# Layer 3 taken ahead of layer 2 as six 512-column products, a copy to rows and eight fp32 transposes, with the tile conversions in two pieces

## The chip, the cores and the metric

The kernel runs on one core of one Trainium2 chip. The metric is the device time of one execution in microseconds (us), and lower is better.

## The reference, cut to what is computed

32 batches of 64 rows and 1024 features go through four residual layers. Two of them are linear layers with a low-rank (LoRA) term, the third multiplies by one of eight 1024x1024 matrices, the fourth mixes the 64 rows of a batch by one of sixteen 64x64 matrices:

```
x = x + (x @ W0.T + b0 + scale[id] * (x @ A0[id].T) @ B0[id])     # ids 1 to 7
x = x + (x @ W1.T + b1 + (x @ A1[id].T) @ B1[id])                 # ids 6 to 15
x = x + x @ W2[id].T                                              # 1024x1024, ids 3 to 7
x = x + einsum('bct,bcd->bdt', x, W3[id])                         # 64x64 on the rows, ids 0 to 15
```

The third layer ("layer 2" in the kernel, counted from 0) acts on features and the fourth ("layer 3") on rows, so the two can be done in either order.

## The kernel before, in words

**Prologue (0 to about 165 us).** Layers 0 and 1 are fused: the product M of their weights, the coupled LoRA tables and the bias are computed once. The batches are sorted by their layer 2 matrix, and tables in SBUF say which batch, LoRA and matrix comes when.

**Pairs.** 16 pairs of batches (128 rows each) follow. Every fp32 operand of a large product is split in a high and a low fp32r part, and a product is three matmuls (hi*hi, hi*lo, lo*hi; `SPLIT`). A 1024-wide result needs two banks of 512 columns, so a product over 8 feature tiles is 8*3*2 = 48 matmuls of 512 columns. For pair j TensorE (PE) does:

- `low_products(j)` (L1056, 8 matmuls of 256 columns): both LoRA A products;
- `main_part(0)` (L1064, 24 matmuls);
- `between_loras(j)` (L1071, one matmul): the first LoRA's contribution to the second's low-rank input. It waits for `low_ready` (the split sums of the first LoRA, DVE L819 to L839) and `g_ready` (`couple`, DVE L807);
- `main_part(1)` (24 more) and `lora_b(j)` (L1079 and L1080, 4 matmuls). `lora_b` waits for the second LoRA's sums (DVE L852 to L839, the second chain). Then `y_done(j)`;
- `layer2(j-1)`: first half (L1101, 24 matmuls with tiles 0 to 3 of the matrix in `ring`), then `transposes(j)`, then the second half (24, tiles 4 to 7).

`transposes(j)` (L1092) does layer 3 and the transpose in one: the stationary operand is a 128x128 block of the split x2, the moving one the 128x128 W3, so 8 blocks * 3 parts = 24 matmuls of 128 columns write `t_ps`, which is already transposed as layer 2 wants it. `x2` is layer 1's output: DVE adds the bias (`take_x2`, L864, after `y_done`), ACT casts the high part (`x2_hi`, L565), DVE the low part (`x2_lo`, L872). The result is split again, half by half: `xs2_hi` (ACT L559), `xs2_lo` (DVE L868).

**The ring.** `ring` holds the current matrix, split, 8 tiles. When the next pair takes the next matrix (`following`), ACT and DVE convert its tiles (`convert`, ACT L547, DVE L859) from a stage of four slots, tiles 0 to 3 in `step(j)` (after layer 2's first half is used) and tiles 4 to 7 in `step(j+1)`. SyncE (SP) loads tile k of 4 to 7 (L277) when the low part of tile k-4 is converted, and in its queue the next pair's loads stand behind them: x (L246), LoRA A (L255), LoRA B (L264 to L267), W3 (L272). The matrix changes four times: three times between pairs (`following`) and once inside a pair (`mixed`).

**Order.** Each engine has its program written by hand, in order; waits are on semaphores. ACT in `step(j)`: `take_out(j-2)`, `xs2_hi(j-1, 1)`, tiles 4 to 7 if due, `a_hi(j+1)` (L527, needs the LoRA A load), `split_w3(j)` (L571), `x_hi(j+1)` (L520, two), `x2_hi(j)`, `b_hi_parts(j+1)` (L534, L535, and the copies L538 and L541, which raise `b_again`), mixed tiles, `xs2_hi(j, 0)`, tiles 0 to 3 if due. DVE follows the same order with its low parts, and the LoRA sums of pair j stand at the start of its step.

## Time and profile before

| | us |
|---|---|
| median of 3 runs | 619.14 (618.62 to 619.67) |
| the profiled execution | 617.97 |
| its span, first to last instruction | 616.2 |
| PE, matmuls busy | 598.6 (97%) |
| PE, weight loads busy | 496.5 (81%) |
| DVE busy | 304.2 (49%) |
| ACT busy | 263.9 (43%) |

"Busy" of PE is the time with a matmul in flight. Matmuls overlap: one of 512 columns is shown with about 390 ns, but the next starts about 230 ns after it. A late matmul is therefore read from the distance of two starts, and the idle time in brackets behind a row is shorter than the delay.

### The profile page before, as it was taken

Reading aid. Unit: us, or ns where it says so; the run is one execution under the profiler, and the core shown is the slowest. Engines: PE = TensorE matmul, PEld = TensorE weight load, DVE = VectorE, ACT = ScalarE, POOL = GpSimd, SP = SyncE. Lnnn points to the kernel's source line nnn. Section 1 sums busy time; section 2 is a strip of 40 time slices with the busy share of each in tenths; the row PEclk is TensorE's granted clock in tenths of the full one; section 3 lists DMA queues with packets and bytes.
Section 4 is the critical chain, followed back from the end, with each engine's and each line's share of the span. In section 5 each row is a group of like instructions: output and inputs, shape, how many; then the busy total and the mean of one; then the engine's idle time right before and its main releaser. Section 6 shows DMA issues by size and latency. Waiting matters only on the chain.

```text
span 616.2 us, 10822 instructions
## 1 busy us (share of the span) xinstructions
PE 598.6 (97%) x2870; PEld 496.5 (81%) x2871; DVE 304.2 (49%) x547; ACT 263.9 (43%) x337; POOL 56.6 (9%) x87
## 2 busy tenths in 40 slices
PE   8999999999989999999999899999999998999997
PEld 7888878888878887888888788888878874888885
DVE  6993220031686368453545845454584563535320
ACT  5632211033485184544527553552755372345111
POOL 3240001000012002000200200020021001000000
PEclk9999999999989999999999999999999997999999
DMA  8646723010054125423121642312164242021102
GB/s 312 236 170 68 86 87 139 18 52 17 2 207 158 53 48 194 172 70 98 41 68 36 204 172 70 98 41 68 36 204 172 70 155 84 17 87 36 36 1 69
DMA packets 66012, 60.92 MB, mean 99 GB/s; under 512 B 42050, under 2 KB 50242, under 8 KB 65988
## 3 DMA queue, kind: packets, MB, share of 16 engines
q1 hardware_dynamic: 65988, 60.63, 33.1%
q8 instruction: 11, 0.18, 0.1%
q14 instruction: 13, 0.11, 0.1%
HBM read 49.33 MB, written 11.27 MB: 98 GB/s over the span
## 4 chain that ended last, share of the span: by engine, by line
PE 79%; issue 6%; DVE 5%; ACT 4%; DMA 2%; ACTq 1%; DVEq 1%; POOL 1%; SPq 0%; POOLq 0%
PE y_ps L1064 22%; PE y_ps L1101 22%; PE y_ps L1018 11%; PE t_ps L1018 5%; PE t_ps L1092 5%; DVE ring L859 2%; PE y_ps L999 2%; PE low_ps L1056 2%; DMA arena<-wt 2%; ACTq L224 1%; PE y_ps L995 1%; PE t_ps L999 1%; PE low_ps L999 1%; ACT ring L547 1%; DVE arena L864 1%
## 5 line engine op out<-in xcount | busy, mean ns | idle before, releaser
L1101 PE MATMUL y_ps<-ring,ops 128*128 128x512 f32 (+1 forms) x792 | 190.3, 396 | 7.1 <-DVE ring L859 4.2
L1101 PEld LDWEIGHTS y_ps<-ring,ops 128*128 128x128 f32 (+1 forms) x792 | 145.8, 186 | 44.4 <-issue 7.9
L1064 PE MATMUL y_ps<-wm,ops 128*128 128x512 f32 x768 | 180.5, 393 | 0.0
L1064 PEld LDWEIGHTS y_ps<-wm,ops 128*128 128x128 f32 x768 | 142.7, 189 | 29.3 <-DVE arena L864 0.2
L1018 PE MATMUL y_ps<-ring,wm 128*128 128x512 f32 x240 | 55.3, 390 | 0.0
L859 DVE TENSOR_TENSOR ring<-arena,ring 128x1024 fp32r<-128x1024 f32 x40 | 48.9, 1271 | 12.2 <-ACT ring L547 12.0
L1018 PEld LDWEIGHTS y_ps<-ring,wm 128*128 128x128 f32 x240 | 44.9, 188 | 9.3
L520 ACT CAST ops<-arena 128x512 fp32r<-128x512 f32 x32 | 19.4, 620 | 70.3 <-PE y_ps L1064 70.3
L547 ACT CAST ring<-arena 128x1024 fp32r<-128x1024 f32 x40 | 40.4, 1049 | 15.9 <-POOL arena L431 15.8
L1092 PEld LDWEIGHTS t_ps<-w_split,ops 128*128 128x128 f32 x384 | 45.9, 194 | 1.2
L431 POOL TENSOR_TENSOR arena<-arena,ident 128x128 f32<-128x128 f32 x40 | 24.5, 622 | 236.6 <-DMA arena<-wt 233.3
L1092 PE MATMUL t_ps<-w_split,ops 128*128 128x128 f32 x384 | 45.4, 275 | 0.0
L577 ACT COPY arena<-y_ps 128x1024 f32<-128x1024 f32 (+1 forms) x17 | 16.4, 964 | 67.4 <-PE y_ps L1101 40.8
L868 DVE TENSOR_TENSOR ops<-t_ps,ops 128x512 fp32r<-128x512 f32 x32 | 22.0, 691 | 45.6 <-ACT ops L559 45.1
L783 DVE TENSOR_TENSOR ops<-arena,ops 128x512 fp32r<-128x512 f32 x32 | 21.7, 687 | 31.9 <-ACT ops L520 31.9
L435 POOL TENSOR_TENSOR w_stage<-w_stage,ident 128x128 f32<-128x128 f32 x16 | 14.2, 886 | 241.1 <-DMA w_stage<-w 241.1
L565 ACT CAST ops<-arena 128x1024 fp32r<-128x1024 f32 x16 | 16.8, 1050 | 45.0 <-DVE arena L864 45.0
L819 DVE TENSOR_TENSOR low_a<-low_ps,low_mask 64x128 f32<-64x128 f32 x32 | 9.2, 288 | 51.7 <-PE low_ps L1056 51.2
L538 ACT CAST ops<-arena 32x1040 fp32r<-32x1040 f32 x32 | 33.9, 1059 | 0.6
L541 ACT CAST b_split<-arena 32x1024 fp32r<-32x1024 f32 x32 | 33.4, 1044 | 0.6
L1018 PE MATMUL t_ps<-ring,wm 128*128 128x512 f32 x144 | 33.3, 390 | 0.0
L1018 PEld LDWEIGHTS t_ps<-ring,wm 128*128 128x128 f32 x144 | 27.0, 188 | 5.6
(142 smaller groups left out, 565.6 us busy)
## 6 DMA issues: line engine op xcount, KB each, us to landing
arena<-wt SPq DMA_DIRECT2D x48, 512.0 KB, 4.6
arena<-xt SPq DMA_DIRECT2D x32, 256.0 KB, 2.8
out<-arena SPq DMA_DIRECT2D x30, 256.0 KB, 3.1
arena<-w SPq DMA_DIRECT2D x8, 576.0 KB, 5.3
a_stage<-a_tab SPq DMA_DIRECT2D x64, 64.0 KB, 1.9
arena<-b_tab SPq DMA_DIRECT2D x64, 64.0 KB, 2.0
arena<-a_cols SPq DMA_DIRECT2D x8, 256.0 KB, 4.1
a_tab<-bias SPq DMA_DIRECT2D x4, 256.0 KB, 8.5
```

The lines of the kernel that those rows point to most:

```text
L431: nc.gpsimd.tensor_tensor(diag, diag, ident[:, :], ALU.add).then_inc(w_folded, 1)
L538: op = nc.scalar.copy(b0_split[group(0, g), :], b0_stage[group(0, HI), :])
L541: op = nc.scalar.copy(b1_split[group(1, g), :], b1_stage[group(1, HI), 0:FEATS])
L547: nc.scalar.copy(ring[:, k, 0, :], w_stage[:, k % STAGES, :]).then_inc(w_hi, 1)
L783: nc.vector.tensor_tensor(xs_of(h, 1), x_of(h), xs_of(h, 0), ALU.subtract).then_inc(x_lo_ready, 1)
L859: nc.vector.tensor_tensor(ring[:, k, 1, :], w_stage[:, k % STAGES, :], ring[:, k, 0, :], ALU.subtract).then_inc(w_lo, 1)
L868: nc.vector.tensor_tensor(xs2_of(h, 1), t_of(h), xs2_of(h, 0), ALU.subtract).then_inc(xs2_lo_ready, 1)
L999: op = nc.tensor.matmul(PASS1[i], wm[:, i, part_w, k * P:(k + 1) * P], a1[:, k, part_a, :], start=False, stop=k == KT - 1 and part_w == 1)
L1018: op = nc.tensor.matmul(to[:, cols], left(part_w, k), ring[:, k, part_r, cols], start=k == 0 and part_w == part_r, stop=k == KT - 1 and pa ...
L1064: op = nc.tensor.matmul(y_ps[:, cols], xs[:, k, part_x, :], wm[:, k, part_w, cols], start=k == 0 and part_x == part_w, stop=False)
L1092: op = nc.tensor.matmul(t_ps[:, cols], x2_split[:, part_x, cols], w3_split[:, part_w, :], start=part_x == part_w, stop=part_x == 1)
L1101: op = nc.tensor.matmul(y[0:m, cols], xs2[:, k, part_x, 0:m], ring[:, k, part_w, cols], start=k == 0 and part_x == part_w, stop=k == KT - ...
```

## The change

PE takes layer 3 as a product of its own ahead of the second half of layer 2: W3 is the stationary operand and x2 the moving one, 2 banks * 3 parts = 6 matmuls of 512 columns (`layer3`). Its result stands in rows; ACT copies it to SBUF as fp32 (`take_x4`, into the place of x2), and eight fp32 transposes of PE bring it into `t_ps`. These stand ahead of the last tile's matmuls of layer 2. The copies that raise `b_again` are a function of their own and move behind `xs2_hi(j, 0)` on ACT; `couple` moves into the next step on DVE. Of tiles 4 to 7, tile 4 is converted ahead of the second LoRA chain's end and tiles 5 to 7 behind it. The first two pairs have an order of their own. SP and GpSimd are as before.

```diff
@@ scalar
-                for g in (A_LO, LOW_LO):
-                    op = nc.scalar.copy(b0_split[group(0, g), :], b0_stage[group(0, HI), :])
-                op.then_inc(b_again, 1)
...
+            def b_again_parts(layer):
+
+                split, stage = ((b0_split, b0_stage), (b1_split, b1_stage[:, 0:FEATS]))[layer]
                 for g in (A_LO, LOW_LO):
...
+                    op = nc.scalar.copy(split[group(layer, g), :], stage[group(layer, HI), :])
                 op.then_inc(b_again, 1)
...
+            def take_x4(j):
+                act.wait_ge(l3_done, j + 1)
+                nc.scalar.copy(x4, t_ps[:, :]).then_inc(x4_ready, 1)
...
+            def first_half_of_next(j):
+                rank, mixed, following = first_rank(act, j), mixed_of(act, j), following_of(act, j)
+                with act.If(following != 0):
+                    act.wait_ge(half_used, j + 1)
+                    convert(rank + mixed + 1, FIRST_HALF)
...
+            def second_step():
+                a_hi(2)
+                convert(0, (6, 7))
+                x_hi(2, 0)
+                take_x4(0)
+                x_hi(2, 1)
+                for h in range(2):
+                    xs2_hi(0, h)
...
+            def step(j, last=False):
+                take_out(j - 2)
+                xs2_hi(j - 1, 1)
+                second_half_of_next(j - 2, SECOND_HALF[:1])
                 if not last:
                     a_hi(j + 1)
...
                 split_w3(j)
+                second_half_of_next(j - 2, SECOND_HALF[1:])
...
                 x2_hi(j)
                 if not last:
                     b_hi_parts(j + 1)
...
+                take_x4(j)
+                behind_layer2(j - 1)
                 xs2_hi(j, 0)
...
+                if not last:
+                    for layer in range(2):
+                        b_again_parts(layer)
+                first_half_of_next(j - 1)
@@ vector
             def take_x2(j):
                 dve.wait_ge(y_done, j + 1)
+                if not (isinstance(j, int) and j == 0):
+                    dve.wait_ge(t_done, j)
...
+            def step(j, last=False):
+                sum_low(j, 0)
+                split_low(j, 0)
+                couple(j)
+                sum_low(j, 1)
+                xs2_lo(j - 1, 1)
+                second_half_of_next(j - 2, SECOND_HALF[:1])
+                finish_low(j)
                 if not last:
                     a_lo(j + 1)
...
                 split_w3(j)
+                second_half_of_next(j - 2, SECOND_HALF[1:])
...
                 take_x2(j)
                 x2_lo(j)
                 if not last:
                     b_lo_parts(j + 1)
...
+                behind_layer2(j - 1)
                 xs2_lo(j, 0)
...
+                first_half_of_next(j - 1)
@@ tensor
+            def layer3(j):
...
+                for cols in BANKS:
+                    for part_x, part_w in SPLIT:
+                        op = nc.tensor.matmul(t_ps[:, cols], w3_split[:, part_w, :], x2_split[:, part_x, cols],
+                                              start=part_x == part_w, stop=part_x == 1)
+                op.then_inc(l3_done, 1)
+
+            def transposes(j):
+                pe.wait_ge(x4_ready, j + 1)
                 for k in range(KT):
                     cols = slice(k * P, (k + 1) * P)
...
+                    op = nc.tensor.transpose(t_ps[:, cols], x4[:, cols], ident[:, :])
                 op.then_inc(t_done, 1)
...
+                    if between and k == KT - 1:
+                        between()
...
-                    layer2(j - 1, lambda: transposes(j))
+                    layer2(j - 1, lambda h: (layer3, transposes)[h](j))
```

Three places show the moved order. The first is PE's loop body, `layer2(j-1)` where the matrix does not change inside the pair. Before:

```order
L1101 MATMUL y_ps<-ring,ops 128x512 x24
L1092 MATMUL t_ps<-w_split,ops 128x128 x24
L1133 REGISTER_ALU
L1134 REGISTER_ALU
L1101 MATMUL y_ps<-ring,ops 128x512 x24
```

The same place now (L1175 is the layer 2 matmul, L1157 layer 3, L1165 the transpose):

```order
L1175 MATMUL y_ps<-ring,ops 128x512 x24
L1157 MATMUL t_ps<-ops,w_split 128x512 x6
L1207 REGISTER_ALU
L1208 REGISTER_ALU
L1175 MATMUL y_ps<-ring,ops 128x512 x18
L1165 MATMUL t_ps<-ident,arena 128x128 x8
L1175 MATMUL y_ps<-ring,ops 128x512 x6
```

The end of the work that writes `t_ps` moved from ahead of the second half to the last tile but one. The second place is ACT at the end of the loop body: the copies behind `b_again` (before L538 and L541), the split of `t_ps` (L559) and the tiles 0 to 3 (L547). Before:

```order
L535 CAST b_split<-arena 32x1024
L538 CAST ops<-arena 32x1040 x2
L541 CAST b_split<-arena 32x1024 x2
...
L559 CAST ops<-t_ps 128x4x128
L616 COMPARE_AND_BRANCH
L546 ISA
L547 CAST ring<-arena 128x1024
```

Now (copies L542, copy to rows L558, split L564, tiles L548, L225 the loads of the table):

```order
L536 CAST b_split<-arena 32x1024
L558 COPY arena<-t_ps 128x1024
...
L564 CAST ops<-t_ps 128x4x128
L542 CAST ops<-arena 32x1040 x2
L542 CAST b_split<-arena 32x1024 x2
L225 TENSOR_LOAD table
...
L599 COMPARE_AND_BRANCH
L547 ISA
L548 CAST ring<-arena 128x1024
```

The four copies now stand between the split of `t_ps` and the tiles. The third place is DVE from the end of one step into the next: split of `t_ps` (now L901), tiles 0 to 3 (L890), then the first LoRA chain (L856 to L876) and `couple` (L844):

```order
L901 TENSOR_TENSOR ops<-t_ps,ops 128x4x128
...
L890 TENSOR_TENSOR ring<-arena,ring 128x1024
L923 UNCONDITIONAL_BRANCH
L1012 REGISTER_ALU
L1012 COMPARE_AND_BRANCH
L856 TENSOR_TENSOR low_a<-low_ps,low_mask 64x128
L858 TENSOR_TENSOR low_sum<-low_ps,low_mask 64x128
L864 TENSOR_TENSOR low_sum<-low_sum,low_a 64x128
L873 CAST low_split<-low_sum 64x128
L874 CAST low_split<-low_sum 32x128
L876 TENSOR_TENSOR low_split<-low_sum,low_split 32x128
L844 TENSOR_TENSOR g_split<-g_mask,ops 128x32
```

Before, the same place had the same order of tiles and chain, without the last row:

```order
L859 TENSOR_TENSOR ring<-arena,ring 128x1024
L916 UNCONDITIONAL_BRANCH
L946 REGISTER_ALU
L946 COMPARE_AND_BRANCH
L819 TENSOR_TENSOR low_a<-low_ps,low_mask 64x128
L821 TENSOR_TENSOR low_sum<-low_ps,low_mask 64x128
L827 TENSOR_TENSOR low_sum<-low_sum,low_a 64x128
L836 CAST low_split<-low_sum 64x128
L837 CAST low_split<-low_sum 32x128
L839 TENSOR_TENSOR low_split<-low_sum,low_split 32x128
```

So on DVE the chain stands behind the four tiles in both kernels; what changed is when ACT reaches the tiles.

## Rows read from the trace of the kernel before

**Rows 1.** The page, busy time and share of the span.

```profile
PE 598.6 (97%) x2870; PEld 496.5 (81%) x2871; DVE 304.2 (49%) x547; ACT 263.9 (43%) x337; POOL 56.6 (9%) x87
```

**Rows 2.** Waits of PE: us in total, times, longest us.

```profile
PE y_ps L1101 <- DVE ring L859: 4.2, 2, 2.9
PE y_ps L1101 <- issue: 2.9, 4, 0.8
PE y_ps L1079 <- DVE low_split L839: 2.2, 3, 1.0
PE low_ps L1071 <- DVE low_split L839: 1.6, 1, 1.6
```

**Rows 3.** Timeline of PE, 325.4 to 355 us: start, us, what, count [idle before].

```profile
325.48 5.60 PE L1101 MATMUL y_ps<-ring,ops 128*128 128x512 f32 x24
330.92 2.79 PE L1092 MATMUL t_ps<-w_split,ops 128*128 128x128 f32 x24
333.54 5.71 PE L1101 MATMUL y_ps<-ring,ops 128*128 128x512 f32 x24
...
345.52 0.22 PE L1071 MATMUL low_ps<-low_split,g_split 128*128 128x128 f32 x1
345.57 5.68 PE L1064 MATMUL y_ps<-wm,ops 128*128 128x512 f32 x24
352.25 0.50 PE L1079 MATMUL y_ps<-ops,low_split 128*128 128x512 f32 x1 [0.99 <-DVE low_split L839]
...
354.25 0.96 PE L1101 MATMUL y_ps<-ring,ops 128*128 128x512 f32 x3 [0.80 <-issue]
```

**Rows 4.** Timeline of ACT, the same stretch.

```profile
330.51 2.13 ACT L538 CAST ops<-arena 32x1040 fp32r<-32x1040 f32 x2
...
334.79 0.59 ACT L559 CAST ops<-t_ps 128x512 fp32r<-128x512 f32 x1
335.40 3.90 ACT L547 CAST ring<-arena 128x1024 fp32r<-128x1024 f32 x4
...
350.58 0.71 ACT L527 CAST side<-a_stage 128x256 fp32r<-128x256 f32 x2 [0.91 <-DMA a_stage<-a_tab]
...
351.39 1.13 ACT L520 CAST ops<-arena 128x512 fp32r<-128x512 f32 x2
```

**Rows 5.** Timeline of DVE, the same stretch.

```profile
326.14 1.23 DVE L864 TENSOR_TENSOR arena<-y_ps,bias 128x1024 f32<-128x1024 f32 x1
328.49 1.22 DVE L872 TENSOR_TENSOR ops<-arena,ops 128x1024 fp32r<-128x1024 f32 x1 [1.11 <-ACT ops L565]
...
332.73 0.20 DVE L807 TENSOR_TENSOR g_split<-g_mask,ops 128x32 fp32r<-128x32 f32 x1 [0.35 <-DVE b_split L799]
...
336.49 4.63 DVE L859 TENSOR_TENSOR ring<-arena,ring 128x1024 fp32r<-128x1024 f32 x4 [0.39 <-ACT ring L547]
341.03 0.28 DVE L819 TENSOR_TENSOR low_a<-low_ps,low_mask 64x128 f32<-64x128 f32 x1
...
342.45 0.28 DVE L839 TENSOR_TENSOR low_split<-low_sum,low_split 32x128 fp32r<-32x128 f32 x1
...
345.90 5.17 DVE L859 TENSOR_TENSOR ring<-arena,ring 128x1024 fp32r<-128x1024 f32 x4 [1.52 <-ACT ring L547]
```

**Rows 6.** Timeline of SP's queue (DMA issues), the same stretch.

```profile
337.89 3.72 SPq L277 DMA_DIRECT2D arena<-wt  x4
...
347.25 1.89 SPq L255 DMA_DIRECT2D a_stage<-a_tab  x4
```

**Rows 7.** Groups of PE: line, what, count | busy us, mean ns | idle.

```profile
L1092 PE MATMUL t_ps<-w_split,ops 128*128 128x128 f32 x384 | 45.4, 275 | 0.0
```

**Rows 8.** Timeline of PE, the 11 fp32 warm-up matmuls.

```profile
1.56 5.06 PE L961 MATMUL y_ps<-ident 128*128 128x128 f32 x22 [1.56 <-POOL ident L404]
```

**Rows 9.** Two stretches by windows: us, busy (count) per engine, granted clock, DMA, GB/s.

```profile
181.30:184.70 3.40, 3.40 (x13) 3.01 (x13) 3.26 (x9) 3.40 (x7) 0.00 (x0) 0.50 0.21 61
...
512.40:519.20 6.80, 6.11 (x15) 3.26 (x16) 1.32 (x2) 0.58 (x1) 0.00 (x0) 0.50 0.28 78
```

More of the change, by code:

```diff
@@ L631, in _ @@
             b_hi_parts(0)
+            for layer in range(2):
+                b_again_parts(layer)
             take_m(6)
@@ new lines, in behind_layer2, with first_half_of_next, first_step @@
+            def behind_layer2(j):
+                rank, mixed = first_rank(dve, j), mixed_of(dve, j)
+                with dve.If(mixed != 0):
+                    convert(rank + 1, range(KT))
+            def first_half_of_next(j):
+                rank, mixed, following = first_rank(dve, j), mixed_of(dve, j), following_of(dve, j)
+                with dve.If(following != 0):
+                    convert(rank + mixed + 1, FIRST_HALF)
+            def first_step():
+                sum_low(0, 0)
+                split_low(0, 0)
+                sum_low(0, 1)
+                convert(0, (0, 1))
+                finish_low(0)
+                a_lo(1)
+                split_w3(0)
+                x_lo(1, 0)
+                convert(0, (2, 3))
+                x_lo(1, 1)
+                take_x2(0)
+                sum_low(1, 0)
+                split_low(1, 0)
+                b_lo_parts(1)
+                couple(1)
+                sum_low(1, 1)
+                x2_lo(0)
@@ new lines, in second_step @@
+            def second_step():
+                convert(0, (4, 5))
+                finish_low(1)
+                a_lo(2)
+                convert(0, (6, 7))
+                for h in range(2):
+                    x_lo(2, h)
+                for h in range(2):
+                    xs2_lo(0, h)
+                split_w3(1)
+                take_x2(1)
+                x2_lo(1)
+                b_lo_parts(2)
+                behind_layer2(0)
+                xs2_lo(1, 0)
+                first_half_of_next(0)
@@ L900, in step @@
                 if not last:
-                    x_lo(j + 1, 0)
-                    if before == 0:
-                        convert(0, (2, 3))
-                    x_lo(j + 1, 1)
+                    for h in range(2):
+                        x_lo(j + 1, h)
                 take_x2(j)
@@ L908, in step @@
                     b_lo_parts(j + 1)
[L909 to L914 removed]
+                behind_layer2(j - 1)
                 xs2_lo(j, 0)
[L916 to L917 removed]
+                first_half_of_next(j - 1)
             masks()
@@ L1058, in low_products, with main_part @@
                 op.then_inc(low_done, 1)
-            def main_part(h):
+            def main_part(h, between=None):
                 for k in (FIRST_HALF, SECOND_HALF)[h]:
+                    if between and k == KT - 2:
+                        between()
                     for part_x, part_w in SPLIT:
```

159 lines of the change are left out of this document (62 added, 97 removed).

## The prediction, made before the changed kernel was run

> **What bounds the kernel now.** I read four views: the page for the share of each engine, the waits of TensorE (PE), the timeline engine by engine around one change of the layer 2 matrix, and windows for the granted clock. PE has a matmul in flight 97% of the span [rows 1], and its waits by the bracketed idle times add up to a few us [rows 2]. In the stretch shown the reader sees PE going from layer 2's first half into the 24 small products, into the second half and on without a gap, until it stands late twice, at 352.25 and 354.25 [rows 3]. So PE is the bound: what leaves PE is gained, and a new wait of PE is lost in full. ACT and DVE are half idle over the span, but near a change of matrix they work without a pause, and there they decide [rows 4, 5].
>
> Of PE's rates: 24 matmuls of 512 columns from 325.48 to 330.92 are 0.227 us each, 24 of 128 columns from 330.92 to 333.54 are 0.109 each [rows 3].
>
> **Part 1, PE's own work.** Gone per pair: 24 products of 128 columns, 2.62 us. New: 6 of 512 columns, 6 x 0.227 = 1.36, and 8 fp32 transposes of 128x128. The trace of before has no transpose. From below, the nearest row is the product of the same tile size, 0.109 [rows 3]. From above there are two rows: the fp32 warm-ups have 22 records for 11 instructions [rows 8], so an fp32 instruction may take two passes, 0.22 us at 0.109 a pass; and one that waits for its predecessor's end costs the 0.275 that the row of L1092 shows for one [rows 7]. I take 0.109: a transpose only moves data, its tile is as large as L1092's, and the weight load seems to set the pace of such small matmuls (four times the columns take only twice the time). That makes 8 x 0.109 = 0.87, and per pair 1.36 + 0.87 - 2.62 = -0.39, times 16 pairs = **-6.2 us**.
>
> The Trainium skill (TensorE: Matmul & The Clock Gate, Terms) says that trn2's matmul and weight load have a transpose mode that is four times faster for fp32; by that one pass is right and the sum stays. The same page (Part 4: PE-mode transpose) gives about 275 ns for a 128x128 transpose inside a kernel; by that the term would be 1.36 + 2.2 - 2.62 = +0.94 a pair, +15 us in all. No row here has a transpose, so it stays a rival.
>
> **Part 2, waits that go.** At the three changes between pairs, lora_b is late because the second LoRA chain stands behind four tiles on DVE, and layer 2 is late behind it. In the stretch shown: 345.57 + 24 x 0.227 = 351.02, but L1079 starts at 352.25, 1.23 late; four matmuls later L1101 should start at 353.28 and starts at 354.25, 0.97 late [rows 3]. The waits for the three places are 2.2 and 2.9 by bracketed idle [rows 2], each too short by 0.16 (a matmul is shown with 0.39 and hands over after 0.23). I take 5.8 in all. The chain now stands behind one tile, so **-5.8 us**; if it is still a little late, up to 3 of these stay.
>
> **Part 3, the first new wait, at the first LoRA chain.** I carry the change into the stretch of [rows 3, 4, 5]. PE starts layer 3 at 330.92 and has done it at 332.28. Then come 18 matmuls (4.09), eight transposes (0.87): t_ps is ready, with 0.2 for the last one's way out, at 337.4. Before, it was ready at 333.7. PE needs the first LoRA's sums at 332.28 + 0.87 + (345.52 - 333.54) = 345.13.
>
> ACT waits for t_ps with L559, now at 337.5, and reaches its next instruction 0.61 later (334.79 to 335.40 [rows 4]): 338.1. Now the four copies stand there. They took 330.51 to 334.79 = 4.28, so ACT gets to tile 0 at 342.4. DVE starts its part 1.09 after ACT (335.40 to 336.49) and comes out of four tiles 4.54 later (341.03) [rows 4, 5]: 343.5 and 348.0. Only then comes the first chain, 341.03 to 342.73 = 1.70, and couple, 0.20 [rows 5]: 349.9. PE goes on at 350.0 instead of 345.1: **4.9 us late**, three times. Before, the tiles were done at 341.03 and the chain at 342.7, 2.8 ahead of need. Nothing else hides it: PE has nothing to do ahead of L1071, and its later work stands in order behind it.
>
> **Part 4, the second new wait, at layer 3.** SP issues tiles 4 to 7 one by one as the DVE frees slots (L277 [rows 6]), and x and LoRA A of the next but one pair stand behind them in its queue. ACT's L527 (LoRA A) started at 350.58, 9.55 after DVE had left its fourth tile at 341.03, and it waited for that load [rows 4, 5, 6]. That moment is now 348.0, so L527 starts at 357.5. Behind L527 in ACT's order stand split_w3, tiles 5 to 7, x_hi twice and x2_hi, and x2_hi is what layer 3 needs. The way: 0.81 to the end of split_w3 (350.58 to 351.39), about 1.0 for the table look-ups of the new branch (DVE's gap ahead of its branch was 1.5 [rows 5]), DVE 1.09 behind ACT and three tiles x 1.135, two x_lo of 0.64 (an estimate by their ACT partners, 1.13 for two [rows 4]): 357.5 + 0.8 + 1.0 + 1.1 + 3.4 + 1.3 = 365.1. take_x2, x2_hi and x2_lo took 326.14 to 329.71 = 3.57 [rows 5], so x2_lo is there at 368.7. PE, going on at 350.0, needs it after main_part(1) 5.5, lora_b 0.9 and layer 2's first half 5.45, with 0.1 for L1071: at 362.0. **6.7 us late**, three times; between 5 and 8, by what the look-ups and transfers take. In the stretch of before the load was early enough: y_done came at 353.4, three us after L527.
>
> **Part 5, the clock.** The trace has PE at 1.2 GHz (granted clock 0.50) for 3.4 us from 181.3, after PE had waited 1.6 us at L1071 and run small products, and for 6.8 us from 512.4, after a wait of 2.9 [rows 2, 9]. Work in such a stretch takes twice as long: 1.7 and 3.4 us lost. A wait of 4.9 or 6.7 is longer than both. A slow stretch behind the first new wait costs nothing, since the second wait's end is set by ACT and DVE and swallows it; one behind the second costs 1.7 to 3.4. I take 2.5, three times.
>
> **Part 6, the rest.** Ordinary pairs: the copies move behind t_ps, end about 342.4 in the coordinates above, and are needed at 345.1 (couple) and 351 (lora_b); ACT has 2.7 us to spare, so 0. The copy to rows (1.0 us on ACT) lies beside 18 matmuls (4.1 us), so 0; without that cover it would cost 1.0 a pair. Start: the wait of 1.6 at L1071 and its slow stretch may go, but layer2(0) now waits for the transposes and both splits behind them (about 1.7) and perhaps for the copy; 0, give or take 2. The mixed pair: its tiles start earlier by about what PE gains before them, so its two waits stay; 0.3.
>
> **The sum.** Per change of matrix 4.9 + 6.7 + 2.5 = 14.1, times 3 = 42.3. 617.97 - 6.2 - 5.8 + 42.3 + 0.3 = **648.6**; I say 649. The profiled execution is 1.2 below the median of 619.14, so against the median the same sum is 650. Own range of this case: 640 to 657 (part 4 at 5 to 8 gives -5 and +4, the clock -2.4 and +2.7, part 2 up to +3, start 2).
>
> **Rivals.**
> - *The transposes cost two passes or do not overlap.* 0.22 or 0.275 instead of 0.109 adds 0.89 or 1.33 a pair, 14 to 21 us, less what falls in a wait: 662 to 670. For it speak the 22 records of [rows 8]; against it that those are full products. Chance 0.12.
> - *Only the first new wait appears.* If the LoRA A load reached ACT before y_done (at 356.4), it would have to start 6 us sooner behind the tiles than in [rows 6]. The sum is then 617.97 - 6.2 - 5.8 + 3 x (4.9 + 2.5) + 0.3 = 628. Chance 0.11.
> - *Faster, because the tiles do not hold the first chain.* One mechanism: DVE must be out of tile 3 by 345.1 - 1.9 = 343.2, so ACT must start tile 0 by 337.6. That is the point that decides. The order puts t_ps (337.4) and four copies ahead, so it would take the copies running outside ACT's order, or a t_ps that is ready 5 us earlier. If it held, waits 3 and 4 and the clock term are gone: 617.97 - 6.2 - 5.8 = 606. Chance 0.08.
> - *The change does nothing to the time:* gains of 12 against new waits of 12, each under a third of what I work out. Chance 0.02.
>
> **How the numbers follow.** The forecast above has 0.67; the time is its 649. The measurement tells 0.2% (1.2 us) from no change. Faster has the third rival, 0.08; same 0.02; slower the rest, 0.90. The range reaches from 631 to 664: the forecast's own range with its tails, the lower half of the first rival, and most of what lies between it and the second; about 0.2 is outside (606, most of 628, above 664).
>
> **What would show it.** Layer 3 with 6 matmuls in about 1.4 us and the transposes at 0.11 each in one record a piece (two records: first rival). At the three changes of matrix, the row of between_loras late by about 5 with DVE's low_split as releaser, and layer3's row late by about 7 with DVE's x2_lo; on ACT four copies between the split of t_ps and tile 0; LoRA A's cast waiting for its DMA. No wait at lora_b. PE at granted clock 0.50 behind these waits. I am wrong if ACT's tiles start at once after the split of t_ps, if the LoRA A load lands before y_done, or if transposes cost other than 0.11.

## The result, and the profile after

The changed kernel takes 645.52 us (median of 4, 644.26 to 646.27), the kernel before in the same comparison 618.88 (4 runs): a ratio of 1.043, interval 1.040 to 1.045. The profiled execution took 646.27, 28.3 more than that of before. The page of after, first lines of busy time (compare [rows 1]), shows PE down from 97% of the span to 93%, with 3.7 us more of matmuls in flight although it has 160 matmuls fewer; ACT has 15.5 us more, about what the 16 copies to rows take (L558, 16.2 us).

```profile
PE 602.3 (93%) x2710; PEld 494.1 (77%) x2711; DVE 304.4 (47%) x547; ACT 279.4 (43%) x353; POOL 54.7 (8%) x87
```

The waits of PE (compare [rows 2]): us in total, times, longest.

```profile
PE t_ps L1157 <- DVE ops L905: 15.0, 3, 5.1
PE low_ps L1137 <- DVE g_split L844: 14.4, 3, 4.9
PE y_ps L1175 <- DVE ring L890: 4.6, 2, 2.7
```

Layer 3 (L1157) waits three times for x2's low part, `between_loras` (L1137) three times for `couple`, 29.4 us together. The wait at `lora_b` is gone and so is the one of 1.6 at L1071; at the start L1175 now waits for the split of `t_ps`, 1.6 by its bracket.

The timeline of PE around the second change of matrix (compare [rows 3]): start, us, what, count, idle before and its releaser.

```profile
338.67 1.52 PE L1157 MATMUL t_ps<-ops,w_split 128*128 128x512 f32 x6
340.03 4.25 PE L1175 MATMUL y_ps<-ring,ops 128*128 128x512 f32 x18
344.12 1.03 PE L1165 MATMUL t_ps<-ident,arena 128*128 128x128 f32 x8
344.91 1.63 PE L1175 MATMUL y_ps<-ring,ops 128*128 128x512 f32 x6
...
347.33 5.63 PE L1130 MATMUL y_ps<-wm,ops 128*128 128x512 f32 x24
357.75 0.44 PE L1137 MATMUL low_ps<-low_split,g_split 128*128 128x128 f32 x1 [4.79 <-DVE g_split L844]
357.99 7.76 PE L1130 MATMUL y_ps<-wm,ops 128*128 128x512 f32 x24
...
366.50 5.60 PE L1175 MATMUL y_ps<-ring,ops 128*128 128x512 f32 x24
377.20 2.93 PE L1157 MATMUL t_ps<-ops,w_split 128*128 128x512 f32 x6 [5.10 <-DVE ops L905]
```

Six products in 340.03 - 338.67 = 1.36 us, eight transposes in 344.91 - 344.12 = 0.79, 0.099 each. `between_loras` is due at 347.33 + 24 x 0.227 = 352.8 and starts at 357.75. Layer 3 is due at 366.50 + 5.45 = 371.9 and starts at 377.20. ACT, the same stretch (compare [rows 4]):

```profile
345.19 0.58 ACT L564 CAST ops<-t_ps 128x512 fp32r<-128x512 f32 x1 [3.94 <-PE t_ps L1165]
345.80 2.13 ACT L542 CAST ops<-arena 32x1040 fp32r<-32x1040 f32 x2
...
350.08 3.89 ACT L548 CAST ring<-arena 128x1024 fp32r<-128x1024 f32 x4
...
356.47 1.04 ACT L548 CAST ring<-arena 128x1024 fp32r<-128x1024 f32 x1 [1.11 <-POOL arena L432]
365.57 0.71 ACT L528 CAST side<-a_stage 128x256 fp32r<-128x256 f32 x2 [8.06 <-DMA a_stage<-a_tab]
...
367.43 2.95 ACT L548 CAST ring<-arena 128x1024 fp32r<-128x1024 f32 x3 [0.95 <-issue]
```

Between the split of `t_ps` (345.19) and tile 0 (350.08) stand the four copies, and L528, the cast of LoRA A, waits 8.06 us for its load, with tiles 5 to 7 behind it. DVE (compare [rows 5]):

```profile
351.17 4.63 DVE L890 TENSOR_TENSOR ring<-arena,ring 128x1024 fp32r<-128x1024 f32 x4 [4.67 <-ACT ring L548]
355.71 0.28 DVE L856 TENSOR_TENSOR low_a<-low_ps,low_mask 64x128 f32<-64x128 f32 x1
...
357.41 0.19 DVE L844 TENSOR_TENSOR g_split<-g_mask,ops 128x32 fp32r<-128x32 f32 x1
...
368.60 3.50 DVE L890 TENSOR_TENSOR ring<-arena,ring 128x1024 fp32r<-128x1024 f32 x3 [1.32 <-ACT ring L548]
...
373.59 1.22 DVE L897 TENSOR_TENSOR arena<-y_ps,bias 128x1024 f32<-128x1024 f32 x1
375.92 1.23 DVE L905 TENSOR_TENSOR ops<-arena,ops 128x1024 fp32r<-128x1024 f32 x1 [1.11 <-ACT ops L570]
```

DVE leaves tile 3 at 355.8, makes the first chain and `couple` by 357.6, and PE goes on at 357.75. The way to layer 3 ends with x2's low part at 377.15, and PE goes on at 377.20.

The windows of three stretches (compare [rows 9]): the first 3.4 us from the restart of PE behind the first wait, the 6.2 us from just before the restart behind the second, and after that. The columns: stretch, length, busy (count) of PE, PEld, DVE, ACT and POOL, granted clock, DMA share, GB/s.

```profile
357.75:361.16 3.41, 3.41 (x9) 2.73 (x10) 2.10 (x5) 0.00 (x0) 0.91 (x2) 0.50 0.98 357
377.00:383.20 6.20, 6.00 (x15) 4.71 (x16) 2.74 (x4) 1.93 (x2) 0.00 (x0) 0.52 0.92 313
383.20:387.70 4.50, 4.50 (x25) 3.79 (x24) 0.55 (x1) 1.15 (x2) 0.00 (x0) 1.00 0.35 118
```

Finer windows show the granted clock at 0.50 (1.2 GHz) already while PE waits (357.0 to 357.5, 376.5 to 377.0). It stays there up to 362.4 behind the first wait and up to 382.9 behind the second, and is then 1.00 (2.4 GHz). That is 4.7 and 5.7 us of slow work behind the two restarts. 24 matmuls took 7.60 us there instead of 5.45 (357.99 to 365.59), so the first stretch cost 2.2; the second cost 2.8 by the distances of PE's starts.

**Where the 28.3 us came from.** The starts of `low_products`, one row a pair, give the ledger; first after, around the second change, then before, the same pairs.

```profile
320.32 1.11 PE L1120 MATMUL low_ps<-ops,side 128*128 128x256 f32 x8
...
346.38 1.12 PE L1120 MATMUL low_ps<-ops,side 128*128 128x256 f32 x8
...
387.70 1.11 PE L1120 MATMUL low_ps<-ops,side 128*128 128x256 f32 x8
```

```profile
312.57 1.12 PE L1056 MATMUL low_ps<-ops,side 128*128 128x256 f32 x8
...
339.10 1.11 PE L1056 MATMUL low_ps<-ops,side 128*128 128x256 f32 x8
...
367.98 1.11 PE L1056 MATMUL low_ps<-ops,side 128*128 128x256 f32 x8
```

An ordinary pair went from 26.53 to 26.05, 0.48 less. A pair with a change of matrix went from 28.88 to 41.32: 0.48 less by PE's own work, 2.35 less by the waits at `lora_b`, and 15.27 more. Over the execution: 14 pairs x 0.48 is 6.7 less; the old waits at the three changes 6.4 less; the new waits with their slow stretches 45.5 more (15.03, 15.27, 15.15); the start 3.2 less beyond that, the mixed pair 0.9 less. The sum is 28.3.

### The profile page after: what moved, and what is told of

Same layout as the page of the kernel before. It is cut to its first block, busy times and chain, and to the rows that moved or that the text cites. A ratio compares the mean times of both kernels' runs of the same rounds, so it can differ in the third digit from the quotient of the medians.

```text
span 644.5 us, 10993 instructions
## 1 busy us (share of the span) xinstructions
PE 602.3 (93%) x2710; PEld 494.1 (77%) x2711; DVE 304.4 (47%) x547; ACT 279.4 (43%) x353; POOL 54.7 (8%) x87
## 4 chain that ended last, share of the span: by engine, by line
PE 78%; DVE 6%; issue 5%; SPq 3%; ACT 3%; DMA 2%; ACTq 1%; DVEq 1%; POOL 0%; POOLq 0%
PE y_ps L1175 24%; PE y_ps L1130 20%; PE y_ps L1082 10%; PE t_ps L1082 5%; PE t_ps L1157 4%; DVE ring L890 3%; PE y_ps L1063 2%; PE t_ps L1165 2%; PE low_ps L1120 2%; SPq L225 1%; PE y_ps L1059 1%; PE t_ps L1063 1%; PE low_ps L1063 1%; DVE ops L820 1%; DMA a_stage<-a_tab 1%
## 5 line engine op out<-in xcount | busy, mean ns | idle before, releaser
L1175 PE MATMUL y_ps<-ring,ops 128*128 128x512 f32 (+1 forms) x792 | 195.3, 400 | 6.4 <-DVE ring L890 4.6
L1130 PE MATMUL y_ps<-wm,ops 128*128 128x512 f32 x768 | 186.1, 401 | 0.0
L1175 PEld LDWEIGHTS y_ps<-ring,ops 128*128 128x128 f32 (+1 forms) x792 | 149.0, 190 | 42.3 <-DVE ring L890 5.5
L1130 PEld LDWEIGHTS y_ps<-wm,ops 128*128 128x128 f32 x768 | 146.6, 194 | 30.7 <-DVE arena L897 0.2
L901 DVE TENSOR_TENSOR ops<-t_ps,ops 128x512 fp32r<-128x512 f32 x32 | 22.0, 691 | 101.0 <-ACT ops L564 100.9
L890 DVE TENSOR_TENSOR ring<-arena,ring 128x1024 fp32r<-128x1024 f32 x40 | 47.8, 1242 | 28.2 <-ACT ring L548 23.8
L564 ACT CAST ops<-t_ps 128x512 fp32r<-128x512 f32 x32 | 18.7, 588 | 68.4 <-PE t_ps L1165 68.4
L432 POOL TENSOR_TENSOR arena<-arena,ident 128x128 f32<-128x128 f32 x40 | 26.3, 666 | 255.0 <-DMA arena<-wt 251.3
L548 ACT CAST ring<-arena 128x1024 fp32r<-128x1024 f32 x40 | 39.7, 1046 | 11.5 <-POOL arena L432 8.1
L1157 PE MATMUL t_ps<-ops,w_split 128*128 128x512 f32 x96 | 28.6, 439 | 15.0 <-DVE ops L905 15.0
L1157 PEld LDWEIGHTS t_ps<-ops,w_split 128*128 128x128 f32 x96 | 20.1, 213 | 20.4 <-DVE ops L905 16.2
L570 ACT CAST ops<-arena 128x1024 fp32r<-128x1024 f32 x16 | 16.8, 1048 | 41.3 <-DVE arena L897 41.3
L542 ACT CAST ops<-arena 32x1040 fp32r<-32x1040 f32 x32 | 33.9, 1059 | 0.6
L542 ACT CAST b_split<-arena 32x1024 fp32r<-32x1024 f32 x32 | 33.5, 1046 | 0.6
L436 POOL TENSOR_TENSOR w_stage<-w_stage,ident 128x128 f32<-128x128 f32 x16 | 10.7, 666 | 252.5 <-DMA w_stage<-w 252.5
L558 ACT COPY arena<-t_ps 128x1024 f32<-128x1024 f32 x16 | 16.2, 1014 | 33.4 <-PE t_ps L1157 33.4
```

The source lines that it names most:

```text
L432: nc.gpsimd.tensor_tensor(diag, diag, ident[:, :], ALU.add).then_inc(w_folded, 1)
L542: op = nc.scalar.copy(split[group(layer, g), :], stage[group(layer, HI), :])
L548: nc.scalar.copy(ring[:, k, 0, :], w_stage[:, k % STAGES, :]).then_inc(w_hi, 1)
L890: nc.vector.tensor_tensor(ring[:, k, 1, :], w_stage[:, k % STAGES, :], ring[:, k, 0, :], ALU.subtract).then_inc(w_lo, 1)
L901: nc.vector.tensor_tensor(xs2_of(h, 1), t_of(h), xs2_of(h, 0), ALU.subtract).then_inc(xs2_lo_ready, 1)
L1130: op = nc.tensor.matmul(y_ps[:, cols], xs[:, k, part_x, :], wm[:, k, part_w, cols], start=k == 0 and part_x == part_w, stop=False)
```

## The experiments

Every time is a median, beside the kernel before on the same chip (618.1 for e1 to e4, 618.3 for e5 to e8, 619.6 for e9 to e12). All edits are to the loop body of the changed kernel, if nothing else is said; in the diffs several calls stand on one line, and `if not last` is left out.

The theory under test: one chain makes both waits. ACT comes late to tile 0 (late `t_ps`, then the copies), so DVE leaves tile 3 late; that holds the first LoRA chain, and by SP's queue also the LoRA A load, behind which tiles 5 to 7, x and x2 stand. The main rival: the two waits have separate causes, or `t_ps` alone makes them.

**e1_copies_back.** ACT:

```diff
+                b_again_parts(0); b_again_parts(1)
                 take_x4(j)
                 behind_layer2(j - 1)
                 xs2_hi(j, 0)
-                b_again_parts(0); b_again_parts(1)
                 first_half_of_next(j - 1)
```

> The changed kernel with one edit: in the loop body of ACT the four copies behind b_again stand ahead of the copy to rows (take_x4), where the kernel before had them, and no longer between the split of t_ps and tiles 0 to 3. Theory (the copies hold the tiles, the tiles hold the first LoRA chain): ACT comes to tile 0 one block of copies, 4.28 us, sooner, so the first wait falls from 4.9 to about 0.7 us, and the layer 3 wait, whose end hangs on the moment DVE leaves tile 3, ends 4.3 sooner too. Three changes of matrix: 3 x 4.3 = 13 us less than 645.5, so about 632.5 (630 to 636); at layer 3 the wait looks longer than 5.3 (about 7.4), because the slow stretch behind the first wait (2.1 us), which it used to swallow, is gone. Rival A (it is the late t_ps alone, behind the transposes, that makes the first wait): the time stays at 645 and the first wait at 4.9. Rival B (the two waits have separate causes): the first goes, the second stays at 5.3, and the slow stretch goes: 3 x (4.2 + 2.1) = 19 less, 626.

Measured 637.12 (1.0315, 1.027 to 1.036): 8.4 less, not 13. The timeline of ACT, DVE and PE:

```profile
342.03 0.59 ACT L564 CAST ops<-t_ps 128x512 fp32r<-128x512 f32 x1 [1.62 <-PE t_ps L1165]
...
343.90 3.90 ACT L548 CAST ring<-arena 128x1024 fp32r<-128x1024 f32 x4 [1.28 <-issue]
...
344.98 4.63 DVE L890 TENSOR_TENSOR ring<-arena,ring 128x1024 fp32r<-128x1024 f32 x4 [1.64 <-ACT ring L548]
...
351.59 0.30 PE L1137 MATMUL low_ps<-low_split,g_split 128*128 128x128 f32 x1 [1.79 <-DVE g_split L844]
...
370.92 2.93 PE L1157 MATMUL t_ps<-ops,w_split 128*128 128x512 f32 x6 [5.59 <-DVE ops L905]
```

The first wait fell from 4.9 to 2.0, and layer 3's grew from 5.3 to 5.7, as the theory wants of two waits on one chain; rival A (4.9 stays) and rival B (layer 3's wait stays at 5.3 and the time falls to 626) are out. It grew by less than the 2.1 expected because the slow stretch stayed: 24 matmuls behind the first wait took 7.1 us instead of 5.45, 1.7 lost after a wait of only 2.0. And the copies were worth 2.9, not 4.28: tile 0 starts 1.28 behind the split, "issue". In the loop body ACT now reads a pair's table entries there (the L225 loads ahead of the branch); in the changed kernel these reads ran under the copies (tile 0 starts at 350.08, right behind the last of them).

**e2_tiles_together.** ACT converts tiles 4 to 7 ahead of `a_hi`; DVE converts tile 4, then `finish_low`, then tiles 5 to 7, then `a_lo`:

```diff
-                second_half_of_next(j - 2, SECOND_HALF[:1])      # ACT
+                second_half_of_next(j - 2, SECOND_HALF)
                 a_hi(j + 1)
                 split_w3(j)
-                second_half_of_next(j - 2, SECOND_HALF[1:])
```

> The changed kernel with one edit: tiles 4 to 7 stand together again, on ACT ahead of the LoRA A cast, on DVE tile 4, the end of the second LoRA chain, then tiles 5 to 7, ahead of the low part of LoRA A. Theory (tiles 5 to 7 idle behind the LoRA A load, and x2 stands behind them): ACT converts tiles 5 to 7 as they land, at about 358.7, 360.7 and 361.9 in the changed kernel's time, DVE is out at 364.5, and LoRA A, W3, x and x2 follow from the load's arrival at 365.6: x2's low part at about 372.4 instead of 377.2. The layer 3 wait falls from 5.3 to about 0.5 (up to 3 if x and x2 are slower than I think) and its slow stretch of 2.4 may go; the first wait stays at 4.9. Total 3 x 4.8 to 3 x 7.2 less: 624 to 631, I say 628. Rival (the load alone sets layer 3, or the tiles cost DVE the same wherever they stand): layer 3 stays 5 us late and the time at 645.

Measured 631.58 (1.0204, 1.016 to 1.025), 0.6 above the span given. Layer 3's wait went from 5.3 to between 2.3 and 2.8, the first stayed at 4.9, so the order of ACT and DVE, not the load alone, makes 2.5 to 3 us of the second wait.

**e3_chain_first.** On DVE `first_half_of_next` moves from the end of the step behind `sum_low(j, 1)` of the next, so the first chain and `couple` stand ahead of tiles 0 to 3:

```diff
                 sum_low(j, 0); split_low(j, 0); couple(j); sum_low(j, 1)
+                first_half_of_next(j - 2)
                 xs2_lo(j - 1, 1)
...
                 xs2_lo(j, 0)
-                first_half_of_next(j - 1)
```

> The changed kernel with one edit, on DVE alone: the first LoRA chain and couple stand ahead of tiles 0 to 3 and no longer behind them. Theory (the moment at which DVE leaves tile 3 sets layer 3, through SP's loads): the first wait, 4.9, goes altogether, but tiles 0 to 3 leave DVE no sooner (355.8 in the changed kernel's time, ACT leads by its own order), so layer 3 starts when it did; its wait grows to about 10, in part shown as a wait of 2 at lora_b. The time stays: 645, at most 3 more or 5 less. Rival (the first wait is a cost of its own): 3 x 4.9 less and the slow stretches behind it, 626 to 631.

Measured 647.58 (1.0459, 1.042 to 1.050). PE's waits of this run:

```profile
PE t_ps L1157 <- DVE ops L905: 22.0, 3, 8.1
PE y_ps L1145 <- DVE low_split L876: 7.9, 3, 2.7
```

The first wait is gone, and nothing is gained: 22.0 us at layer 3 instead of 15.0, and 7.9 at `lora_b`. Counted from the start of `main_part(0)`, DVE leaves tile 3 even later, at 9.7 us instead of 8.5, and the three pairs take 0.4 to 1.6 us more each. This is the clearest sign that the first wait alone was no cost of its own: the moment at which DVE leaves tile 3 decides.

**e4_loads_first.** SP issues x and LoRA A of the next but one pair ahead of tiles 4 to 7:

```diff
                     load_a(which)
+                    following_chunks(j - 2)       # tiles 4 to 7, from the end of the step before
                     sp.wait_ge(b_lo, 2 * j + 2)
```

> The changed kernel with one edit, in SP's queue alone: x and LoRA A of the next but one pair are issued ahead of tiles 4 to 7 instead of behind them. ACT and DVE keep their order. Theory (the LoRA A load, queued behind the tiles' loads, is what ACT waits 8 us for): that wait goes, LoRA A's cast starts behind tile 4, tiles 5 to 7 follow as they land, and layer 3's wait falls from 5.3 to between 0.5 and 3 us; the tiles' loads now start a few us later since SP issues six loads and reads their numbers first. The first wait stays 4.9. Total 624 to 637, I say 632. Rival (ACT waits for the tiles' own loads and folding, whatever SP's order): the wait only moves from LoRA A to the tiles, and the time stays at 645.

Measured 634.2 (1.0244, 1.020 to 1.029), inside the span given. ACT of this run, in the same change of matrix:

```profile
350.70 1.04 ACT L556 CAST ring<-arena 128x1024 fp32r<-128x1024 f32 x1 [0.99 <-POOL arena L440]
351.65 0.71 ACT L536 CAST side<-a_stage 128x256 fp32r<-128x256 f32 x2
358.00 0.30 ACT L584 CAST w_split<-w_stage 128x128 fp32r<-128x128 f32 x1 [5.64 <-POOL w_stage L444]
```

The 8 us in front of LoRA A's cast are gone, and layer 3's waits are 1.6, 3.1 and 3.4. What remains is the rival in part: W3's split now waits 5.64 for POOL, which folds W3 behind the tiles, and tiles 5 to 7 stand behind it.

**e5_tiles_first.** On ACT `first_half_of_next` ahead of `xs2_hi(j, 0)`, on DVE ahead of `xs2_lo(j, 0)`:

```diff
                 behind_layer2(j - 1)
+                first_half_of_next(j - 1)
                 xs2_hi(j, 0)                      # DVE: xs2_lo(j, 0)
-                first_half_of_next(j - 1)
```

> The changed kernel with one edit on ACT and one on DVE: tiles 0 to 3 stand ahead of the first split of t_ps (right behind the copy to rows), the split and the four copies behind them. Tiles 5 to 7 stay behind the LoRA A cast. Theory (the moment DVE leaves tile 3 decides both waits): ACT starts tile 0 about 1.2 us behind the copy to rows, at 342.4 instead of 350.1 in the changed kernel's time, DVE leaves tile 3 at about 348.1 instead of 355.8, and the first wait (4.9) goes wholly. LoRA A's cast comes 9.8 behind that moment and x2's low part 11.6 behind the cast, 369.5 instead of 377.2; PE needs it at 364.8, so a layer 3 wait of about 4.7 stays. Total 3 x 7.7 = 23 less: 622 (619 to 629, if look-ups cost more). Rival (t_ps and its transposes decide, since the split still waits for them): DVE is held by the split of t_ps instead, the first wait stays at 2 or more, and the time is above 632.

Measured 625.1 (1.011, 1.008 to 1.014), inside the span given. The first wait is gone (0.0 at all three), layer 3's is 4.2 to 4.5, and 1.0 stands behind `lora_b`: 20 us less for moving two calls.

**e6_all_three.** e5 with e1's copies and e2's tiles.

> The changed kernel with three edits: tiles 0 to 3 ahead of the split of t_ps, the four copies back ahead of the copy to rows, tiles 4 to 7 ahead of the LoRA A cast (with the end of the second LoRA chain behind tile 4 on DVE). Theory: the first wait is gone; layer 3's wait is 2 us, since the run with tiles 4 to 7 together had x2's low part 3 us sooner after DVE left tile 3; no slow stretch, or a shorter one, behind it. 3 x 10.2 to 3 x 12.6 less than 645.5, and 1.2 more in the mixed pair: 609 to 616, I say 612, which is 1% below the kernel before. Rival (six products and eight transposes cost more than 24 small ones wherever they stand, or the copy to rows crowds ACT): not below the kernel before, 618 or more.

Measured 618.88 (1.0001, 0.998 to 1.002): no different from the kernel before, 3 above the span I gave. DVE and PE:

```profile
345.48 1.51 DVE L889 TENSOR_TENSOR ring<-arena,ring 128x1024 fp32r<-128x1024 f32 x1 [1.55 <-issue]
...
349.69 3.50 DVE L889 TENSOR_TENSOR ring<-arena,ring 128x1024 fp32r<-128x1024 f32 x3 [1.57 <-issue]
...
355.29 1.22 DVE L896 TENSOR_TENSOR arena<-y_ps,bias 128x1024 f32<-128x1024 f32 x1
...
357.63 1.23 DVE L904 TENSOR_TENSOR ops<-arena,ops 128x1024 fp32r<-128x1024 f32 x1 [1.11 <-ACT ops L570]
...
358.91 2.14 PE L1156 MATMUL t_ps<-ops,w_split 128*128 128x512 f32 x6 [2.98 <-DVE ops L904]
```

Layer 3 still waits 3.1, and with it come slow stretches that I had not counted (the granted clock is 0.65 for 3.4 us from 358.9); the mixed pair takes 46.18 instead of 43.64. There ACT comes to its eight tiles 1.9 us later, behind the copies, and the first wait is 3.9 instead of 2.0; but the second is 0.8 shorter, and 1.5 of the 2.5 lost lies in a slow stretch behind the first, so the copies alone don't explain the total (see e11). The rows show DVE without a pause of its own but for two of "issue", 1.55 ahead of tile 4 and 1.57 ahead of tiles 5 to 7. Each is a reading of three table entries, which the kernel before did once here.

**e7_before_order.** The six products and transposes with all four tiles 4 to 7 ahead of `finish_low` on DVE, as before, and e5's place for tiles 0 to 3:

```diff
                 xs2_lo(j - 1, 1)
-                second_half_of_next(j - 2, SECOND_HALF[:1])
+                second_half_of_next(j - 2, SECOND_HALF)
                 finish_low(j)
                 a_lo(j + 1)
                 split_w3(j)
-                second_half_of_next(j - 2, SECOND_HALF[1:])
```

> The changed kernel's layer 3 (six products, copy to rows, eight transposes) with the tiles in the kernel before's order on both engines: four tiles together ahead of the end of the second LoRA chain; tiles 0 to 3 ahead of the split of t_ps, copies behind it. Theory (the change's gain on PE is real and its loss is the order alone): no first wait, no layer 3 wait; the waits at lora_b and behind it, 2.1 us a change in the kernel before, are back (2 to 3). Ordinary pairs 26.05 instead of 26.53. The kernel before less 16 x 0.48 = 7.7, less about 3.5 at the start and the mixed pair, and up to 3 back for tiles that start later: 607 to 614, I say 610. Rival (splitting tiles 4 to 7 around the second chain is worth its 2.4 us a change even here): this comes out 3 us or more above the run with all three edits.

Measured 620.92 (1.0037, 1.002 to 1.006): 7 above the span, a miss. `lora_b` waits 3.6 at each change instead of 0.4 to 1.2, with up to 1.0 behind it, and slow stretches follow. It comes out 2.0 above e6, short of the rival's 3. The gain of the products does not come by itself; the second chain behind four tiles is worse here than in the kernel before, because tile 4 comes later: DVE starts it 3.3 us behind `between_loras` in this run (349.10 and 345.75), in the kernel before 0.4 behind [rows 3, 5].

**e8_transposes_early.** PE:

```diff
-                    if between and k == KT - 1:
+                    if between and k == KT - 2:
                         between()
```

> The changed kernel with one edit, on PE alone: the eight transposes stand one tile (six matmuls, 1.36 us) earlier in layer 2's second half, behind 12 matmuls instead of 18. The copy to rows still has 2.7 us of cover for its 1.0 and its start of 0.2, so no pair waits for it. Theory (ACT waits for t_ps, then copies, then tiles): everything behind t_ps comes 1.36 sooner, first wait 4.9 to 3.6 and layer 3 sooner by as much: 3 x 1.36 = 4 less, 641.4 (639 to 643). Rival (the copies alone hold the tiles and t_ps is early enough): 645. A copy that is not covered any more would show as a new wait in all 16 pairs, 0.8 each, 650 or more.

Measured 638.18 (1.0334, 1.030 to 1.037). The first wait is 3.5 as expected (4.9 - 1.36); ordinary pairs stay at 26.05, so the copy to rows is covered by 12 matmuls. The time fell by 7 instead of 4: by the distances of PE's starts the slow stretches cost 1.6 or 1.7 in four of six places (2.4 and 2.6 in the others) instead of 2.1 to 2.9, and the mixed pair took 1.6 less. With the 4.1 expected that is 8.6 of the 9.4 by which the two profiled executions differ; why the stretches were shorter is not shown. The late `t_ps` is one part of the first wait, the copies the other.

**e9_one_lookup.** e6, and a pair's entries are read once for each place:

```diff
+                facts = facts_of_pair(j - 2)
-                second_half_of_next(j - 2, SECOND_HALF[:1])
+                second_half_of_next(j - 2, SECOND_HALF[:1], facts)
                 finish_low(j)
-                second_half_of_next(j - 2, SECOND_HALF[1:])
+                second_half_of_next(j - 2, SECOND_HALF[1:], facts)
```

> The run with all three edits, and one more on ACT and DVE: the table entries of a pair (rank, mixed, following) are read once for tile 4 and tiles 5 to 7, and once for the mixed tiles and tiles 0 to 3, instead of once for each. Theory (what was left in that run is DVE's own queue: tile 4 at 345.48 after 1.55 of issue, tiles 5 to 7 at 349.69 after 1.57 of issue, then LoRA A, x, x2 without a pause): the second look-up of 1.57 goes, layer 3's wait falls from 3.1 to 1.5, and the slow stretch behind it (1.6 us lost) may go. 3 x 1.6 to 3 x 3.2 less than that run's 618.9: 609 to 614, I say 611. Rival (the LoRA A load, which landed at 349.7, sets DVE's end, and the look-ups are hidden behind it): no change, 618.

Measured 610.21 (0.9861, 0.983 to 0.989). DVE and PE:

```profile
344.87 3.50 DVE L893 TENSOR_TENSOR ring<-arena,ring 128x1024 fp32r<-128x1024 f32 x3
...
352.81 1.23 DVE L908 TENSOR_TENSOR ops<-arena,ops 128x1024 fp32r<-128x1024 f32 x1 [1.11 <-ACT ops L570]
...
354.09 1.65 PE L1165 MATMUL t_ps<-ops,w_split 128*128 128x512 f32 x6 [1.44 <-DVE ops L908]
```

Tiles 5 to 7 start at once behind the chain, layer 3 waits 1.6, and the granted clock stays at 1.00 behind it:

```profile
354.09:357.50 3.41, 3.41 (x15) 2.84 (x16) 2.72 (x3) 3.35 (x4) 0.26 (x1) 1.00 0.36 113
```

The pairs with a change fell from 32.0, 31.4 and 31.3 to 28.7 each, 8.6 for a reading of three words in three places, with the slow stretches it brought; the mixed pair gave 1.4. The edit also takes out a second reading, ahead of tiles 0 to 3, but that one gave nothing: DVE leaves tile 3 2.0 us behind the start of `main_part(0)` in e6 and in e9. The rival is out: the LoRA A load came to ACT at the same place in the pair, 11.7 and 11.8 behind that start.

**e10_x2_sooner.** e9, and on DVE:

```diff
                 split_w3(j)
+                take_x2(j)
                 x_lo(j + 1, 0); x_lo(j + 1, 1)
-                take_x2(j)
                 x2_lo(j)
```

> The run with one look-up, and on DVE the bias add of x2 (take_x2) ahead of x's two low parts instead of behind them; ACT's cast of x2 then runs while DVE makes x's low parts (1.28 us). Theory: x2's low part comes 1.2 sooner, layer 3's wait is 0.5 or less, no slow stretch behind it. 3 x (3.1 - 0.4) + 3 x 1.6 = 13 less than the run with all three edits: 606 (603 to 610), 2% below the kernel before. In ordinary pairs nothing changes (26.05). Rival (ACT's cast is late too, behind its x casts, or y_done sets x2): no less than the run with one look-up.

Measured 604.87 (0.9779, 0.975 to 0.981), as expected and the fastest of all. Its page, and two of PE's waits:

```profile
PE 587.4 (97%) x2710; PEld 483.2 (80%) x2711; DVE 301.2 (50%) x547; ACT 279.3 (46%) x353; POOL 56.3 (9%) x87
```

```profile
PE y_ps L1183 <- DVE ring L893: 6.1, 2, 3.3
...
PE t_ps L1173 <- ACT arena L558: 1.0, 3, 0.4
```

The pairs with a change of matrix take 27.05 instead of 41.3, 1.0 above an ordinary pair; half of that is a wait of the transposes for the copy to rows. The largest waits left are those of the mixed pair (6.1 us for its tiles).

**e11_mixed_copies.** e10, and in the mixed pair ACT makes the copies behind its tiles:

```diff
-                b_again_parts(0); b_again_parts(1); take_x4(j); behind_layer2(j - 1, facts)
+                with act.If(facts[1] != 0):
+                    take_x4(j); convert_mixed(facts[0], j - 1); b_again_parts(0); b_again_parts(1)
+                with act.Else():
+                    b_again_parts(0); b_again_parts(1); take_x4(j)
```

> The run with x2 sooner, and in the mixed pair ACT makes the four copies behind its eight tiles instead of ahead of them (the copy to rows first). Theory: the mixed pair took 46.18 us with the copies ahead of the tiles and 43.64 with them behind; the mixed pair gets about 2.5 back and nothing else moves, so 2 to 3 us below the run with x2 sooner: 603.5. Rival (the mixed pair is bound by its tiles' loads and folding): the first of its two waits shrinks and the second grows by as much, no change.

Measured 606.12 (0.9798, 0.977 to 0.983): nothing gained, the rival's case. The mixed pair took 45.36 instead of 45.09; its first wait went from 3.4 to 1.6 and its second from 3.0 to 4.3, since the later tiles wait for their loads. The start was 1.2 longer, with PE waiting for the copy to rows of the first pair; the edit doesn't touch that place, and I have no cause for it.

**e12_products_kept.** The kernel before, DVE alone: tile 4, `low(j, 1)`, tiles 5 to 7 with one reading, and `take_x2` ahead of x's low parts (the diff leaves the last out).

```diff
                     xs2_lo(j - 1, 1)
-                    second_half_of_next(j - 2)
+                    second_half_of_next(j - 2, SECOND_HALF[:1], facts)
                 low(j, 1)
+                    second_half_of_next(j - 2, SECOND_HALF[1:], facts)
```

> The kernel before, with its 24 products of 128 columns and ACT's order untouched; on DVE alone the second chain's end stands between tile 4 and tiles 5 to 7 (one look-up for both), and take_x2 ahead of x's low parts. It leaves layer 3 as it was, so it shows what the order gives without the six products. Theory: the waits at lora_b and behind it, 2.1 us a change of matrix, go: 3 x 2.1 = 6 less than 618.3, 612 (610 to 615); ordinary pairs stay at 26.53. The run with x2 sooner stays 5 to 8 below this one, by 16 x 0.48 on PE and 2 at the start, less what waits it keeps. Rival (the order gives all of the gain): both end within 2 us of each other. Another rival (splitting the tiles costs LoRA A and x2 what the chain gains): 618.

Measured 610.95 (0.9871, 0.984 to 0.990). No wait is left at the three changes, all at 26.53. So the order on DVE alone is worth 1.3% in the kernel before. e10 is 6.1 below this run, and not by the products alone: by the starts of `low_products`, PE's own work gives 6.7 (14 pairs x 0.48) and the start, which has an order of its own, 4.7; the three changes give back 2.9 (1.0 each over an ordinary pair, against none here) and the mixed pair 2.4.

## Why the prediction came out as it did

The forecast was 649 in its own coordinates (648.6 against the profiled 617.97); the profiled execution of after took 646.3. Against the median the same sum was 650, and 645.5 was measured. The direction, the two waits and the chain between them were as worked out. One releaser was not as *What would show it* has it: the first wait ends with `couple` (g_split), as Part 3 works it out, and not with low_split. By its steps:

- *Part 1, -6.2.* Measured 0.48 a pair, about 7. A transpose takes one record and 0.099 us; the rival of two passes or 0.275 is out. The record of one transpose is long, though: 272 ns in the mean, as L1092's 275 of [rows 7], and they overlap. The Trainium skill (TensorE: Matmul & The Clock Gate, Part 4: PE-mode transpose) gives about 275 ns in a kernel, next to a figure for bf16; the fp32 trace agrees with it as one instruction's duration and not as its pace.
- *Part 2, -5.8.* Measured -6.4 by the pairs (1.66, 2.35 and 2.37 over an ordinary pair). The forecast read 2.9 in [rows 2] as three places; it is four, the fourth (0.5) in the pair ahead of the first change, and by distances the brackets are 0.17 and 0.24 too short, not 0.16. The two slips partly cancel.
- *Part 3, 4.9 late.* Measured 4.9. The route was right in each point (the split at 345.2, copies, tile 0 4.9 behind the split, chain, `couple`). e1 and e8 confirm its two parts, with one correction: of the copies' 4.28, 1.3 covered the readings of the table, so taking them away gives 2.9.
- *Part 4, 6.7 late.* Measured 5.3, but counted as the forecast counted it, 7.4: the slow stretch behind the first wait delayed PE by 2.2 (24 matmuls from 357.99 to 365.59 instead of 5.45), and the second wait swallowed it, as Part 5 said. LoRA A's cast came 9.8 behind DVE's tile 3 (forecast 9.55), x2's low part 11.6 behind that (11.2). e2 and e4 undid two links of that chain one at a time (tiles behind the cast, load behind the tiles), and each took about 3 us off this wait, not all of it.
- *Part 5, 2.5.* Measured 2.7 to 2.9 behind the second wait, at granted clock 0.50.
- *Part 6, nothing.* Mis-sized, on the good side: the start gave 3.2 and the mixed pair 0.9. At the start the wait of 1.8 at L1071 and its slow stretch of 1.8 went, a wait of 0.6 in the next pair went too, a wait of 1.8 at L1175 came, and the second pair holds two of the layer 3 products, 0.5 more than the 14 x 0.48 counts.

Per change of matrix 15.2 was measured and 14.1 forecast, 3 us in all; the start and the mixed pair gave back 4.4, and parts 1 and 2 gave 1.1 more. That they come out within 2.3 us in sum is in part luck: 3 one way, 5.5 the other. The terms of its range add up to 639 to 660 and not 640 to 657; the measured time is inside both. The rival *faster* named tile 0's start as the point that decides, and e5 and e10 show that it was right in that: with the tiles out in time and the second chain's order mended, the kernel with the same products is 2.2% faster (interval 1.9 to 2.5%). Of that, e12 has 1.3% without the products.

Two things stay open: how e11 lengthened the start, and what a slow stretch costs behind a given wait, since that varied within one execution (in e8 1.7, 2.6 and 1.7 behind three waits of 3.5). So no time here can be split cleanly into waits and clock.

## What to carry to other kernels

A change that takes work from the bound engine is worth what the engines feeding it can still deliver: here 0.48 a pair was gained and 15.2 a change lost, because a late input and four copies now stood ahead of four tiles on ACT, and the tiles, as before, ahead of a short chain on DVE (1.9 us) that PE waited for. Look at which long, patient work stands in front of short, urgent work in each in-order queue, follow also what the queue's last item releases (here a DMA queue with the next pair's loads), and count a reading of three control words as 1.3 to 1.6 us unless the engine still has long work queued ahead of it. If removing one wait gains nothing, as in e3, it was not the head of its chain.

## What the runs showed of the hardware

- Reading three table words before a branch stopped DVE for 1.55 us (e6) and ACT for 1.3 (e1), shown as "issue"; behind four queued copies on ACT it cost nothing (tile 0 at 350.08 in the changed kernel). Taking one out of DVE's critical stretch gave 8.6 us in three changes, slow stretches included (e9).
- A wait on PE can cost more than itself: behind the 4.9 and 5.2 us waits shown above the granted clock was 0.50 for 4.7 and 5.7 us, 2.2 and 2.8 us lost, and behind the waits of 2.0 in e1 1.7 were lost each time. The length of the wait alone doesn't tell: behind the 1.6 us waits of e9 the clock stayed at 1.00, while in the kernel before a wait of 1.6 at L1071 was followed by a stretch at 0.50 [rows 9], and in e10 nothing was lost behind a wait of 3.4 in the mixed pair (granted clock 1.00).
- Eight fp32 transposes of 128x128 follow each other at 0.099 us though each is shown with 0.272.
